# Order of score tiles within a visit: two exponent tiles, two maxima tiles, one exponent tile, one maxima tile

## The reference

```python
q = split_heads(x @ w_q)                       # 8 batches, 20 heads of 16, 512 queries
k, v = split_heads(text @ w_k), split_heads(text @ w_v)          # 1593 text tokens
out_text = softmax(q k^T / sqrt(16)) v
k_ip, v_ip = split_heads(ip @ w_k_ip), split_heads(ip @ w_v_ip)  # 8 more tokens
out_ip = softmax(q k_ip^T / sqrt(16) + mask_ip) v_ip
out = (merge(out_text) + merge(out_ip)) @ w_out + b_out + x
```

## Time and profile before

| | us |
|---|---|
| median of 3 runs | 1841.0 (1839.46 to 1841.32) |
| the profiled execution | 1848.91 |
| its span, first to last instruction | 1847.0 |
| PE busy | 1811.4 (98%) |
| DVE busy | 1332.3 (72%) |
| ACT busy | 1185.7 (64%) |
| POOL busy | 382.6 (21%) |
| mean granted TensorE clock, share of full | 0.993 |

### The profile page before, as it was taken

One profiled execution on the slowest core, in us unless ns is written; L12 is line 12 of the kernel. 1 busy time (PEld: TensorE's weight loads), 2 busy tenths in 40 slices (PEclk: granted clock), 3 DMA queues, 4 the chain that ended last, 5 costly groups with the idle time before them and its releaser, 6 DMA issues.

```text
span 1847.0 us, 41069 instructions
## 1 busy us (share of the span) xinstructions
PE 1811.4 (98%) x16856; PEld 718.8 (39%) x16856; DVE 1332.3 (72%) x1787; ACT 1185.7 (64%) x2340; POOL 382.6 (21%) x508
## 2 busy tenths in 40 slices
PE   8999999999999999999999999999999999999988
PEld 3333333433344343433344333343333433434332
DVE  6777777778767787677876777777777777767871
ACT  1276666666666666666666666666666666666766
POOL 5112222211122121122121221112122122221000
PEclk9999999999999999999999999999999999999989
DMA  7555334363344434355453464435544364343410
GB/s 226 102 92 160 67 77 92 73 164 73 74 106 116 106 71 86 94 139 102 79 99 75 141 103 77 97 69 144 94 77 96 72 155 85 74 95 74 77 30 26
DMA packets 103806, 178.16 MB, mean 96 GB/s; under 512 B 42933, under 2 KB 71270, under 8 KB 103618
## 3 DMA queue, kind: packets, MB, share of 16 engines
q1 hardware_dynamic: 82658, 134.12, 37.3%
q0 software_dynamic: 18944, 40.10, 6.9%
q10 hardware_dynamic: 2016, 1.31, 0.2%
HBM read 117.63 MB, written 48.98 MB: 90 GB/s over the span
## 4 chain that ended last, share of the span: by engine, by line
PE 93%; DMA 2%; DVE 2%; SPq 1%; ACT 1%; issue 1%; POOL 0%; ACTq 0%; DVEq 0%; POOLq 0%
PE pv_bank L800 27%; PE max_bank L727 20%; PE work_bank L582 12%; PE exp_bank L784 12%; PE work_bank L604 11%; PE work_bank L627 3%; PE work_bank L593 2%; PE max_bank L745 2%; PE exp_bank L788 1%; DVE tile_max L1069 1%; DMA o_t<-o_sum 1%; SPq L475 1%; ACT probs L978 1%; PE work_bank L658 1%; PE work_bank L611 1%
## 5 line engine op out<-in xcount | busy, mean ns | idle before, releaser
L978 ACT ACTIVATE probs<-exp_bank 128x512 f32<-128x512 f32 x1908 | 1002.0, 599 | 417.3 <-PE exp_bank L784 410.2
L1069 DVE TENSOR_REDUCE tile_max<-max_bank 128x2 f32<-128x1024 f32 x632 | 773.4, 1224 | 400.5 <-PE max_bank L727 395.5
L727 PE MATMUL max_bank<-k_stack,q_stack 48*128 48x512 f32 x1896 | 567.9, 469 | 7.4 <-DVE tile_max L1069 7.3
L800 PE MATMUL pv_bank<-probs,v_ones 128*17 128x512 f32 x3840 | 518.1, 603 | 0.1
L1071 DVE TENSOR_REDUCE tile_max<-max_bank 128x1 f32<-128x512 f32 x632 | 430.2, 681 | 2.7 <-PE max_bank L727 2.7
L784 PE MATMUL exp_bank<-q_stack,k_stack 50*128 50x512 f32 x1908 | 415.9, 403 | 4.0 <-DMA q_stack<-neg_rows 2.7
L727 PEld LDWEIGHTS max_bank<-k_stack,q_stack 48*128 48x128 f32 x1896 | 234.0, 185 | 409.8 <-issue 269.6
L784 PEld LDWEIGHTS exp_bank<-q_stack,k_stack 50*128 50x128 f32 x1908 | 240.0, 188 | 63.2 <-ACT probs L978 47.2
L582 PE MATMUL work_bank<-ctxt,wk 128*32 128x400 f32 x2528 | 253.5, 506 | 7.6 <-DMA wk<-in_w_k 5.5
L604 PE MATMUL work_bank<-wv,ctxt 128*32 128x320 f32 x3040 | 254.0, 435 | 0.0
L604 PEld LDWEIGHTS work_bank<-wv,ctxt 128*32 128x32 f32 x3040 | 93.8, 109 | 163.1 <-issue 100.3
(11 more groups left out here) (124 smaller groups left out, 832.3 us busy)
## 6 DMA issues: line engine op xcount, KB each, us to landing
k_stack<-scratch_k SPq DMA_DIRECT2D x234, 199.2 KB, 6.9
scratch_k<-k_parts SPq DMA_DIRECT2D x80, 400.0 KB, 4.6
ctxt<-in_ctx_t POOLq DMA_DIRECT2D x28, 800.0 KB, 11.1
q_stack<-scratch_q SPq DMA_DIRECT2D x240, 64.0 KB, 2.3
scratch_q<-q_parts SPq DMA_DIRECT2D x80, 128.0 KB, 5.7
r_wide<-scratch_r POOLq DMA_DIRECT2D x39, 256.0 KB, 5.1
xres<-in_x SPq DMA_DIRECT2D x8, 640.0 KB, 9.0
out<-xres SPq DMA_DIRECT2D x32, 160.0 KB, 1.9
```

What stands on the lines that cost most here:

```text
L727: nc.tensor.matmul(round_place(n, r)[:, k, :], exact(q_stack[stack, slot, c, t * 128:(t + 1) * 128]), exact(k_stack[stack, slot, c, chunk ...
L800: last = nc.tensor.matmul(pv_bank[h * 32:h * 32 + VW, :], v_ones[:, v_slot(b, kt), head * VW:(head + 1) * VW], p, start=(kt == 0), stop=(k ...
L978: nc.scalar.activation(dst, exp_place(group_no, at), ACT.Exp, scale=SCALE).then_inc(probs_ready, 1)
L1069: nc.vector.reduce_max(flat[:, at:at + 2], place[:, 0:2, :], AX.X).then_inc(max_taken, 1)
```

## The change

Only the order in which TensorE issues the six tiles of a visit changes. Before: two maxima tiles, three exponent tiles, one maxima tile. Now: two exponent tiles, two maxima tiles, one exponent tile, one maxima tile. The waits move along with the tiles that they stand before: the one for `neg_loaded` in visit 0, which stood before the first exponent tile, now comes first in the visit, and the one for `max_taken` comes behind two exponent tiles. The programs of the other engines stay as they are.

```diff
                     for v in range(VISITS):
                         n, r = round_at(group_no, v)
-                        if n is not None and r:
-                            max_round(n, r)
+
                         if v == 0:
                             pe.wait_ge(neg_loaded, (group_no + 1) * 32)
                         if v < VISITS - 1:
-                            for at in exp_turn(group_no, v):
+                            for at in exp_turn(group_no, v)[:2]:
+                                exp_tile(group_no, at)
+                        if n is not None and r:
+                            max_round(n, r)
+                        if v < VISITS - 1:
+                            for at in exp_turn(group_no, v)[2:]:
                                 exp_tile(group_no, at)
                         if n is not None:
                             if r:
```

## The result

| | before | after |
|---|---|---|
| median, us (4 runs each) | 1840.37 (1839.46 to 1841.32) | 1868.12 (1867.52 to 1873.1) |
| ratio | | 1.0145, 95% interval 1.0125 to 1.0165 |
| profiled execution, us | 1848.91 | 1867.88 |
| its span, us | 1847.0 | 1866.1 |

The account below looks back on a forecast made before the run. PE's own work bounds the kernel, with VectorE's reductions nearest to delaying it. Seven batches at 2.53 us (17.7), 0.7 in the last batch and 3.5 for light rows make 21.9 us on 1841.0: 1863, range 1852 to 1873.

Parts of the forecast that it names:

- visits of 2.4 us and more have the same length: Sign for the profile after: longer visits keep their length, as lateness up to 0.47 us into the next visit costs nothing.
- kind 0: visits 14 and 16: Small matmuls in visit 14 and exponent tiles in visit 16 already wait for the single reduction: 0.23 us each per batch.
- kind 1: visit 13: Behind light visit 12 of 1.88 us, the single maxima tile's load comes later: 0.23 us per batch.
- kind 2: visit 3: Late ACT delays visit 2's second exponent tile and so the reductions; visit 3's single tile loads late: 0.28 us per batch.
- kind 3: visits 5, 8, 13; 10: Single tile loads late behind visits of 1.88 us, 0.23 us each, and behind visit 9 of 2.12 us, 0.09.
- kind 4: the same: Late loads behind light visits 4, 7 and 12, 0.23 us each, and behind visit 9, 0.09 us.
- DVE and ACT busy times stay: Sign for the profile after: the busy times of VectorE and ACT don't change; no size given.
- the term for the ends of the program: Rows of light visits in the first two groups and last batch pay some 15 times 0.23, 3.5 us.
- Rival 1: Extra meetings of tiles on one array half expose 0.19 us weight loads in about 545 visits: 100 us, 1941; chance 0.01.
- Rival 2: ACT holds the visit after a light one; earlier exponents save 0.09 us in about 57 visits: 1836 us; chance 0.03.
- Rival 3: No change: the reductions catch up by an earlier single one or a hidden pause on VectorE; 1838 to 1844; chance 0.05.
- Rival 4: More 1.2 GHz stretches near the end, plus full price in visits under 2.3 us: 1875; chance beyond the range 0.03.

Follow-up runs that it names:

- e2_long_only: The kernel before with the new order only in visits that are not short (57 of 75 in a steady batch); 1842.48 us, ratio 1.0002.
- e3_after_half: The changed kernel with VectorE's single reduction reading 256 of its 512 elements; 1837.02 us, ratio 0.9976 to the kernel before.
- e4_before_half: The kernel before, old order, with VectorE's single reduction reading 256 of its 512 elements; 1833.5 us, ratio 0.9958.
- e9_first_only: The kernel before with the new order only in group 1, the second group of the first batch; 1841.36 us, ratio 1.0002.
- e7_before_fill: The kernel before with one K projection chunk moved from visit 5 to light visit 4 in kinds 3 and 4; 1840.76 us, ratio 1.0.

## Why the prediction was right, and where it was short

**The mechanism held, step by step.** The reductions moved by 0.23 to 0.24 us; the single one ended at 2.63 (2.62 predicted); the load came 0.80 into the next visit and the product at 1.22, both as written. The sign "visits of 2.4 us and more have the same length" was badly put, since the cost falls on the visit behind, and visits 8 (2.51) and 14 of kind 0 (3.83) were to grow by the prediction's own sum. What held is that nothing grew behind a visit of 2.4 us or more. e2_long_only and the pair e3_after_half and e4_before_half show that the rest of the order costs little or nothing.

**The sum by its terms**, per steady batch, medians of the growth of each visit:

| term | predicted | measured |
|---|---|---|
| kind 0: visits 14 and 16 | 0.23 + 0.23 | 0.24 + 0.23 |
| kind 1: visit 13 | 0.23 | 0.24 |
| kind 2: visit 3 | 0.28 | 0.30 |
| kind 2: visit 14 | 0 | 0.25 |
| kind 3: visits 5, 8, 13; 10 | 3 x 0.23 + 0.09 | 0.24 + 0.24 + 0.24 + 0.09 |
| kind 4: the same | 3 x 0.23 + 0.09 | 0.23 + 0.23 + 0.23 + 0.10 |
| batch | 2.53 | 2.86 |

**The first step that failed** is "DVE and ACT busy times stay", from which visit 14 of kind 2 had no term. The prediction followed the shift along the reductions and stopped there. It did not ask what comes next on VectorE in visit 14 of kind 2, where the negation now meets GpSimd. That is 7 x 0.25 = 1.8 us of the 5.8 us between the predicted 21.9 and the measured 27.7. The rest of the 0.33 per batch is small differences of the other terms, 0.6 us in all. For groups 3 to 36 the measured terms make 7 x 2.86, less 1.26 for kinds 0 to 2 of batch 0, plus 0.71 for kinds 0 and 1 of the last, 19.5 us; the profiles give 19.4.

**The second is the term for the ends of the program**, 3.5 us for rows of light visits: by its counts 12 of the 31 visits in the first two groups, 1.4 us, and 19 in the last batch, 2.1. The first two groups measured 4.9 us in place of 0.7 (their share of the batch's sum) and 1.4: the late reductions gave 1.6, less than said, and the low clock came on top, for which the sum had no term. In group 37 the term is there: the group takes 39.0 us in after and 37.3 in e9_first_only, e2_long_only and e7_before_fill, 1.7 more (the same 1.7 by visits, 0.5 of them in visits 14 and 16). In group 38 it can't be seen: 37.4 us in after and 38.9, 37.9 and 37.8 in the other three, which differ in their low-clock stretches.

**Rivals.** Rival 1 (meetings) fell with e2_long_only. Its price was counted too low: the change reorders 15 visits in each of 39 groups less one, 584 and not 545, so 111 us by its own load of 0.19. Rival 2 (faster, ACT the holder) had a grain of truth: ACT stood 0.03 us behind VectorE, as e4_before_half shows, but since VectorE was first, earlier exponents brought nothing. Rival 3 (VectorE catches up) fell: the single reduction still starts 1.15 us after the wide one (684.12 to 685.27). Rival 4 (the clock) named the right mechanism at the wrong end of the program: the low stretch of the earlier trace rows near the end was gone in after's profile but for 3.4 us, and a longer one stood at 156 us. The forecast held no term for it, only the range did.

**Still open:** the medians differ by 27.7 us, of which 19.4 are the steady groups, about 5 the first two and 1.7 group 37. The remaining 1.6 or so are not tied to a place; profiles differ by more than that in where group 0 starts. What sets off the long low-clock stretch is open too.

## What to carry to other kernels

When a reduction takes two tiles at once, it is the place of the second tile in the order that counts, and moving it later delays everything behind it on that engine; look for the shortest stage, since there the engine has no time to catch up and the stage after it pays in full. Price such a shift with "lateness of the load less what it may be late for nothing", read from one waiting and one free visit: here this gave each visit that it was used on within 0.02 us. And follow the shift to the end of the delayed engine's program, for it can also change whom its small operations run beside.

## What the hardware showed unexpectedly

- A VectorE operation on 128 x 16 elements took 0.78 us instead of 0.18 when it began 0.10 us after a GpSimd operation of 0.85 us, and ended with it, in all seven places, and in one place of before; begun 0.14 us ahead of it, it took the usual time and GpSimd's was not longer either. The Trainium skill, SBUF — State Buffer, section Who interferes with whom, says that a VectorE instruction with two inputs in SBUF contends with a GpSimd instruction that reads SBUF. The trace agrees: `neg_parts` is made from `neg_max` and `neg_parts`, both in SBUF. The wide and the single reduction, with one input, kept 1224 and 681 ns in the mean.
- Which profile shows a stretch at 1.2 GHz near 156 us, and how long, was not settled by the order of the work alone: 13.65 us in four kernels, none at that place in another with the same order in those groups.
- Two tiles on different halves of the array cost one slot of 0.23 to 0.24 us together in any of the three orders tried, whichever kind of tile stood on a half before them.
